# A graph attention layer on one core: the last pair of heads turned by the DMA queue instead of TensorE

## The reference, cut to what matters

```
q, k, v = x @ wq.T + bq, x @ wk.T + bk, x @ wv.T + bv          # x: 384 x 1024
q2, k2, v2 = (q @ wiq.T + biq), (k @ wik.T + bik), (v @ wiv.T + biv)   # 16 heads of 64
scores = einsum('hnd,hmd->hnm', q2, k2) / 8 + mask             # 384 x 384 a head
attn = softmax(scores, axis=-1)
out = einsum('hnm,hmd->hnd', attn, v2)                         # back to 384 x 1024
y = layernorm(x + out @ wo.T + bo)
```

## Time and profile before

| | |
|---|---|
| three runs, median (lowest to highest) | 294.86 us (294.46 to 295.31) |
| the profiled execution's own time | 295.16 us |
| its span, first to last instruction | 293.4 us |
| granted TensorE clock, mean over the span | 0.994 of full speed |
| PE busy | 286.8 us, 98% |
| PEld / DVE / ACT / POOL busy | 268.0 / 191.6 / 157.6 / 137.9 us |
| last pair's scores end | 251.9 us into the span |
| last product ends | 288.0 us |

### The profile page before, as it was taken

How to read it: one execution, slowest core, us unless ns; L and a number is a source line. 1 busy time by engine, 2 the same in 40 slices (tenths; PEclk the granted TensorE clock), 3 DMA queues, 4 the chain that set the end, 5 groups by cost and what they waited for, 6 DMA issues and landing times.

```text
span 293.4 us, 5231 instructions
## 1 busy us (share of the span) xinstructions
PE 286.8 (98%) x1674; PEld 268.0 (91%) x1674; DVE 191.6 (65%) x481; ACT 157.6 (54%) x304; POOL 137.9 (47%) x122
## 2 busy tenths in 40 slices
PE   8999999999999999999999999999999999999992
PEld 8999999999999988888999999999999998788882
DVE  5889967566766673325167778787868686952184
ACT  5954323442344342421087777777777777673432
POOL 2000745546556551556755354636363637845500
PEclk9999999999999999999999999999999999999997
DMA  7959864472664339845120303131212222410013
GB/s 269 326 155 359 285 203 154 143 214 82 205 216 135 120 108 345 299 143 163 63 71 18 128 25 121 41 103 44 99 59 84 69 74 71 150 69 2 0 71 143
DMA packets 14030, 39.83 MB, mean 136 GB/s; under 512 B 3168, under 2 KB 4032, under 8 KB 13888
## 3 DMA queue, kind: packets, MB, share of 16 engines
q1 hardware_dynamic: 11904, 38.19, 38.5%
q0 software_dynamic: 1680, 0.62, 1.1%
q10 hardware_dynamic: 432, 0.85, 0.8%
HBM read 37.44 MB, written 2.21 MB: 135 GB/s over the span
## 4 chain that ended last, share of the span: by engine, by line
PE 98%; DVE 1%; ACT 0%; issue 0%
PE bank L892 23%; PE bank L883 19%; PE bank L885 18%; PE bank L884 18%; PE bank L998 6%; PE bank L981 5%; PE bank L969 5%; PE bank L908 3%; PE bank L901 1%; ACT res L577 0%; DVE stats L857 0%; DVE res L856 0%; DVE mean_var L859 0%; ACT std L572 0%; DVE zeros L594 0%
## 5 line engine op out<-in xcount | busy, mean ns | idle before, releaser
L354 POOL DMA_INDIRECT mask_cells<-cell_value,cell x48 | 54.9, 1145 | 73.4 <-DMA mask_cells<-cell_value,cell 30.7
L325 POOL TENSOR_TENSOR w_lo<-w_raw,w_hi 128x1024 fp32r<-128x1024 f32 x18 | 42.9, 2404 | 45.5 <-DVE shared L780 40.9
L409 ACT ACTIVATE w_hi<-w_raw 128x1024 fp32r<-128x1024 f32 x49 | 51.3, 1053 | 20.1 <-PE bank L892 15.1
L883 PE MATMUL bank<-x_hi,w_hi 128*128 128x384 f32 x176 | 58.8, 334 | 0.0
L884 PE MATMUL bank<-x_lo,w_hi 128*128 128x384 f32 x176 | 58.8, 334 | 0.0
L885 PE MATMUL bank<-x_hi,w_lo 128*128 128x384 f32 x176 | 58.8, 334 | 0.0
L604 DVE TENSOR_TENSOR w_lo<-w_raw,w_hi 128x1024 fp32r<-128x1024 f32 x31 | 37.8, 1223 | 17.1 <-ACT w_hi L409 16.0
L883 PE MATMUL bank<-h_hi,w_hi 128*128 128x384 f32 x128 | 47.2, 368 | 0.0
L452 ACT ACTIVATE h_hi<-bank,bcol 128x384 f32 (+1 forms) x24 | 14.0, 583 | 54.5 <-PE bank L885 49.2
L885 PE MATMUL bank<-h_hi,w_lo 128*128 128x384 f32 x128 | 43.1, 337 | 0.0
L884 PE MATMUL bank<-h_lo,w_hi 128*128 128x384 f32 x128 | 42.9, 335 | 0.0
(11 more groups left out here) (102 smaller groups left out, 520.9 us busy)
## 6 DMA issues: line engine op xcount, KB each, us to landing
w_raw<-weights SPq DMA_DIRECT2D x53, 512.0 KB
shared<-key_rows SPq DMA_DIRECT2D x6, 512.0 KB
shared<-start SPq DMA_DIRECT2D x5, 320.0 KB, 6.0
res<-x_rows SPq DMA_DIRECT2D x1, 1536.0 KB, 7.2
out<-res SPq DMA_DIRECT2D x6, 256.0 KB, 2.0
mask_cells<-cell_value,cell POOLq DMA_INDIRECT x48
shared<-start ACTq DMA_DIRECT2D x2, 320.0 KB, 5.0
mask_cells<-mask SPq DMA_DIRECT2D x1, 576.0 KB, 6.1
```

The lines of the kernel that those rows point to most:

```text
L325: nc.gpsimd.tensor_tensor(lo, w_raw[:, s, cols], hi.bitcast(F32), ALU.subtract)\
L354: nc.gpsimd.indirect_dma_start(out=mask_cells, out_offset=bass.IndirectOffsetOnAxis(ap=cell[:, c:c + 1], axis=0), in_=cell_value[:, c:c + ...
L409: nc.scalar.activation(w_part(t, s, slice(0, F))[0], w_raw[:, s, :], ACT.Copy).then_inc(w_hi_done, 1)
L883: pe.matmul(out_ps, w_hi[:, s, cols], moving_hi, start=(k == 0), stop=False)
```

## The change

For the last pair alone, the six groups of TensorE transposes go. In their place the probabilities are written as two 16-bit planes and turned by the DMA queue:

- the scores are masked and the exponentials taken as before; `invert` (VectorE, two small operations for a step of rows) makes 32768 / row sum; `high_planes` (ScalarE, one instruction for each of six row tiles) writes the scaled probabilities rounded to fp16; `low_planes` (VectorE, one for each) writes the rest, also fp16;
- SP issues for each of the six row tiles a transposing DMA of the high plane and one of the low plane, 128x384 of 2 bytes each (96 KB), twelve in all; the last weight tile's load (tile 55) stands between the sixth and the seventh;
- when the three row tiles of a head have landed, `turned_high` (ScalarE) and `turned_low` (VectorE) copy, group by group, to `pt_hi` and `pt_lo`; they take the place of `pt_high` and `pt_low`, which read PSUM;
- the results are scaled back by 1/32768 where the halves are added.

For all pairs `vp` has four slots (high, low of each head), so that GpSimd's copy (L335) and the memset of the zeros (L595) go; the odd head's product with `pt_lo` now has 64 weight columns, not 128. The small tables of the graph stage share one `scratch` tensor with the planes. GpSimd's wait L386 goes. And the ending is written in another order:

```
@@ tensor
-            project(0, 2)
-            project(1, 2)
-
-            pe.wait_ge(masked, 2 * NT * PAIRS)
-            transposes(a, 0)
...
-            values(a, 1, 5)
+            for k in range(2, 4):
+                project(0, k)
+                project(1, k)
+
+            pe.wait_ge(masked, 2 * NT * a + 2)
+            for k in range(4):
+                project(2, k, left)
+            for g in range(NT):
+                values(a, 1, g)
+            project(0, 4)
+            project(1, 4)
+            for g in range(NT, 2 * NT):
+                values(a, 1, g)
+            project(0, 5)
+            project(1, 5)
             pe.wait_ge(sum_done, 2 * a + 1)
-            project(2, 0)
-            project(2, 1)
-            project(2, 2)
+            for k in range(4):
+                project(2, k, slice(1, 3))
...
-                for k in range(3, KT):
+                for k in range(4, KT):
                     last = project(2, k, slice(i, i + 1))
@@ sync
+            def turn(place):
+                i = ROW_TILES[place]
+                b, h = divmod(i, 2)
+                sp.wait_ge(plane_hi_done, place + 1)
+                sp.dma_start_transpose(turned_hi[:, h, b, :, :], plane_hi[:, i, :]).then_inc(turned_hi_landed[h], 16)
+                sp.wait_ge(plane_lo_done, place + 1)
+                sp.dma_start_transpose(turned_lo[:, h, b, :, :], plane_lo(i)).then_inc(turned_lo_landed[h], 16)
+
             for t in range(2 * RING, TILES):
+                if t == TILES - 1:
+                    for place in range(NT):
+                        turn(place)
                 load_tile(t, t % RING)
...
+            for place in range(NT, 2 * NT):
+                turn(place)
@@ scalar, the ending
-            exps(a)
+            exps(a, range(0, 3))
+            high_planes(range(0, 2))
+            exps(a, range(3, 4))
+            high_planes(range(2, 3))
+            exps(a, range(4, 5))
+            high_planes(range(3, 4))
+            exps(a, range(5, 6))
+            high_planes(range(4, 6))
...
                 if i == 1:
-                    pt_high(a, (0, 1))
                     att_high(a - 1)
                 if i == 2:
-                    pt_high(a, (4, 5))
-                    att_half_out(a, 0)
+                    turned_high(range(0, NT))
                 if i == 3:
-                    att_half_out(a, 1)
+                    att_half_out(a, 0, scale=1.0 / UP)
+                    turned_high(range(NT, 2 * NT))
+                    att_half_out(a, 1, scale=1.0 / UP)
                     att_high(a)
                 high_part(LAST_TILES + i, i, LAST_TILES // RING + 1)
@@ vector, the new functions and the ending
+            def invert(a, places):
...
+                then_settle(nc.vector.tensor_scalar(row_inv[:, cols], row_sum[:, cols], 1.0 / UP, None, ALU.mult))
+                then_settle(nc.vector.reciprocal(row_inv[:, cols], row_inv[:, cols]))
+            def low_planes(places):
...
+                    nc.vector.scalar_tensor_tensor(out=plane_lo(i), in0=probs[:, i, :], scalar=row_inv[:, i:i + 1],
+                                                   in1=plane_hi[:, i, :], op0=ALU.mult, op1=ALU.subtract)\
+                        .then_inc(plane_lo_done, 1)
+            def turned_low(groups):
...
+                    dve.wait_ge(turned_lo_landed[h], 16 * NT)
+                    dve.wait_ge(pv_done, 2 * NT * (PAIRS - 1) + g - NT + 1)
+                    nc.vector.tensor_copy(pt_lo[:, g % 3, :].rearrange("p (b q) -> p b q", b=NT),
+                                          turned_lo[:, h, :, m, :]).then_inc(pt_lo_done, 1)
...
-            attention(a)
-            pt_low(a, (4,))
...
+            for place in range(4):
+                mask_scores(a, place)
+            invert(a, (0, 1))
+            mask_scores(a, 4)
+            invert(a, (2,))
+            low_planes((0, 1))
+            mask_scores(a, 5)
+            for place in range(NT, 2 * NT):
+                invert(a, (place,))
+                low_planes((place - 1,))
+            low_planes((5,))
+            turned_low(range(0, NT))
+            add_halves(a, 0, scale=1.0 / UP)
+            turned_low(range(NT, 2 * NT))
+            add_halves(a, 1, scale=1.0 / UP)
```

## The result

| | before | after |
|---|---|---|
| four runs each, median (lowest to highest) | 294.85 us (294.46 to 295.31) | **302.45 us** (301.88 to 302.88) |
| ratio, 95% interval | | 1.0255 (1.0242 to 1.0267) |
| profiled execution, its time / span | 295.16 / 293.4 us | 301.88 / 300.1 us |
| granted TensorE clock, mean | 0.994 | 0.987 |
| TensorE: first row behind the scores to last product's end | 251.87 to 288.01, 36.14 us | 251.65 to 294.09, 42.44 us |

The change makes the kernel 7.6 us slower; the forecast was 1.3 us faster. In the chain that ended last SyncE's queue stands with 3%, where the earlier trace rows had none, and VectorE has grown from 1% to 6%.

A forecast was written before the change was run, and what follows sets the result against it. TensorE was taken to bound the ending: 2.0 us of transposes go, VectorE's tail takes 0.75, so the last piece starts 1.25 earlier; from 294.86 the forecast is 293.6 us, range 292.8 to 299.0.

The forecast's parts named there:

- the issue price of a transposing DMA: On SP's queue: each transpose taken at 0.47 us, bounded above by GpSimd's indirect transfers at 0.97 each.
- Stall: nothing: TensorE ahead of the last pair's values: no wait, with slack of 3.3 us (even head) and 4.7 us (odd head).
- Rival 1: SP's queue: twelve issues in a row delay the odd head's values, TensorE waiting from 0.94 us each; 296.7 to 299.7; chance 0.30.
- Its start, 254.0: SP's queue: the first high plane is ready and the first transpose issued at 254.0 us.
- rival 2: VectorE's turned low plane copies held by GpSimd's low parts: 294.8, at most 296.0; chance 0.23 together with a late landing.
- The figure for one block: DMA transposes: 1309 ns per 128x128 block, thirty-six in a row 47 us, or nothing changed if mostly overlapping latency.
- 2.0 us come off TensorE: TensorE behind the scores: six transpose groups and the longer steps after them go, 1.97, say 2.0 us.
- The values were wanted at: TensorE behind the scores: even head's values want their data at 264.3 us, the odd head's at 268.1.
- VectorE becomes the bound of the tail: Output rows at the end: VectorE bounds the last 9 us and takes 0.75 of the 2.0 us.
- Landing, taken as 2.0: Transposing DMAs: data lands 2.0 us after the issue, bounded above by 6.1 us.
- The narrower weights, GpSimd's copy and the memset: Odd heads' 64-column weights, GpSimd's copy and VectorE's memset of zeros: priced at nothing.

The follow-up runs named there:

- noscale: The changed kernel without the multiplication of the row sums by 1/32768: 299.78 us, ratio 1.0164.
- paired: The changed kernel with each row tile's high and low plane side by side, turned by one DMA, six in place of twelve: 294.72 us, ratio 0.9985.
- the filler run: The changed kernel with 18 products that nothing reads added ahead of the odd head's values: 300.24 us, ratio 1.0176.
- four_dmas: `paired` with one-column inversions, earlier even-head copies, tile 55 first, the odd head in one DMA, row 2's feature tile 3 split: 293.30 us, ratio 0.9927.
- tail: The kernel before with row 2's feature tile 3 computed ahead of rows 0 and 1's last tiles: 295.44 us, ratio 1.0015.
- the probe: The kernel before with four-slot values and, in SyncE's queue, unread transposing DMAs of 1 to 12 blocks and two plain copies: 295.05 us.
- tile55_first: The changed kernel with tile 55's load ahead of all twelve transposes instead of behind six: 301.58 us, ratio 1.0197.
- onecol: The changed kernel with the first two inversions done one column at a time: 300.75 us, ratio 1.0179.

## Why the prediction was wrong

**The step that failed is the issue price of a transposing DMA.** "I take 0.47", the row of SyncE's plain transfers, with 0.97 as the upper end for what occurs twelve times. It is 1.18 to 1.28, median 1.25, beyond both. The row of the same queue was taken for the nearer one, but the two kinds differ by operation, not by queue: in one queue, a plain copy of the same bytes issues in 0.55 and a transpose in 1.2. Where the prediction had "Stall: nothing" there are two stops of 6.0 us together; 4.2 of them stand without the late start (`noscale`), and with half the issues 0.7 are left (`paired`). Rival 1 was this mechanism, its place (SyncE's queue) and its point of decision (0.94); by its formula 1.25 gives 294.86 - 1.25 + 3.7 = 297.3.

**Two things lacked in that rival's own sum**, which is why even it fell 5 us short and the time lies beyond the range's 299.0:

- Its start, 254.0. The first issue was at 256.01, since the two-column multiply was held for 2.20 us. The prediction had the mechanism (rival 2, from the earlier trace rows) but put it on the copies of the turned low planes, and priced both operations of an inversion by a row of the reciprocal alone, 0.19 each. The copies ran unheld, three in 1.47 from 264.95, beside GpSimd's low parts of the attention output and of the next tile (264.57 to 270.27). With 256.01 its formula comes to 273.4 for the landing; the trace has 273.28.
- The clock. A stop was priced at its length; the filler run shows 2.2 us more for the stop of 4.27. So 302.45 is, from the median, 294.86 + 6.0 stops + 2.2 clock - 2.0 transposes + 0.6 tail, 301.7; of the 0.75 left, 0.57 is that by which the median lies above the profiled execution.

**The figure for one block.** The Trainium skill, "VectorE: DVE Perf Modes", section on the three transpose paths, has 1309 ns for one 128x128 block by DMA. Here one block issues in 1.19 us and three in 1.21, landing 3.4 and 2.4 after the issue's start: as a price of an instruction the page's figure is near (1.2 to 1.3), as a price of a block it would be three times too high. The prediction read it only as 36 blocks in a row or as latency that overlaps; the reading that held is between the two. The Trainium skill, "GPSIMD Engine Reference", section "Specifications", says that GpSimd shares the SBUF interfaces with VectorE's two-port modes and with its instructions of two SBUF inputs. By that rule the low planes can be held, which the prediction left as unseen: the `noscale` trace agrees, 1.36 us for one that takes 0.62 with GpSimd idle.

**What was right.** 2.0 us come off TensorE (the account closes to 0.1 with it, and `four_dmas` has them). The values were wanted at 264.02 and, from there, on the planned step (264.3 and 268.1 forecast; 264.52 and 268.32 in `four_dmas`). VectorE becomes the bound of the tail, 0.62 in the trace of `tail` (0.42 between the medians) for 0.75. Landing, taken as 2.0, is 2.4. The narrower weights, GpSimd's copy and the memset are worth nothing. VectorE had the sixth low plane at 261.85 for some 260.5, the hold included, so behind the first issue the planes were never the bound: each landing waited for the queue.

## What to carry to other kernels

A transposing DMA is priced by the instruction on the queue that issues it (1.2 us for 1 to 6 blocks here): put several blocks into each, as long as its landing, which grows with the blocks (2.4 us for 3, 3.7 for 12), still comes in time, and multiply the count by the issue before anything else; a row of another kind of transfer in the same queue is no price for it. When a stop of the bottleneck engine is priced, add what its clock loses behind the stop, and look at the start of the chain for small instructions that a second engine can hold. And balance the tail: work moved ahead of the last rows is cover for a wait, but the engine that finishes the rows then sets the end.

## What the runs showed of the hardware

- A DMA transpose of 16-bit data from SBUF to SBUF costs SyncE's queue 1.19 us with 1 block of 128x128, 1.21 with 3, 1.21 with 6 and 1.43 with 12; 2.65 with 18, behind three others. Twelve of 3 blocks in a row take 1.25 each. Landing is 2.4 us for 3 blocks, 2.8 for 6, 3.7 for 12, 4.7 for 18.
- The first transpose behind a weight load of 512 KB lands later: 3.3 and 3.8 us for 2.4 with 3 blocks (the changed kernel), 4.6 for 2.8 with 6 (`paired`), 3.4 for a single block (the probe). With the load moved from the seventh to ahead of the first (`tile55_first`), the seventh lands after 2.4 and the first after 3.8.
- Beside GpSimd's low part a VectorE multiply of *two* columns took 2.20 us, ending when the low part did, but its one-column form 0.15 and a two-column reciprocal 0.16; the 128x384 copies from fp16 to fp32r stepped 0.46 beside it. No run left GpSimd's work out.
- TensorE's clock fell to 1.2 GHz inside a stop of 4.3 us and stayed there for 4.6 us of unbroken work; behind a stop of 1.7 us, at 265.76, it stayed at 2.4 GHz. In `noscale` it was still full at the end of the stop (1.00 over 270.0 to 272.2) and fell just behind it (0.66 over 272.25 to 273.10). How long the lower level lasts varied: until some 276.0 in `noscale` (values from 272.25) and 278.7 in `onecol` (values from 272.87), behind stops of 4.2 and 4.3 us. What sets it was not tried.
